# Group norm and channel attention in fp16 halves: norms from weights times T, shared blocks side by side, and another order in the head

## The reference, cut to what matters

```python
x = x + attention(group_norm(x))        # x: 16 images, 192 channels, 48*48 = 2304 pixels
# group_norm: 32 groups of 6 channels, each image alone
qkv = xt @ w_qkv                        # xt: (2304, 192), w_qkv: (192, 576)
q = q / max(sqrt(sum over pixels of q*q), 1e-12)     # by channel; k likewise
k = k * temperature                     # by head; 8 heads of 24 channels
attn = softmax(k^T q)                   # 24 x 24 for each head: sums over the pixels
out = (v @ attn) @ w_out + b_out
```

## Time and profile before

| | us |
|---|---|
| median of 3 runs | 373.13 (372.38 to 373.38) |
| the profiled execution | 374.76 |
| its span in the profile | 372.8 |
| TensorE busy | 331.2 (89%) |
| VectorE busy | 283.2 (76%) |
| ScalarE busy | 235.9 (63%) |
| GpSimd busy | 150.4 (40%) |

### The profile page before, as it was taken

The page is one execution under the profiler, slowest core; times in us unless marked ns, Lnnn a source line. Parts: engine busy times, 40 slices in busy tenths (PEclk is TensorE's granted clock), DMA queues, the critical chain, the costliest instruction groups (busy, mean ns, idle before and its releaser), DMA issues.

```text
span 372.8 us, 9327 instructions
## 1 busy us (share of the span) xinstructions
PE 331.2 (89%) x3724; PEld 233.4 (63%) x3724; DVE 283.2 (76%) x666; ACT 235.9 (63%) x410; POOL 150.4 (40%) x133
## 2 busy tenths in 40 slices
PE   0048856999999999999999999999999999999795
PEld 0036645875778566865777577856686577765452
DVE  4889855887699669986799769966998665359774
ACT  1098489763997299747996399729974699610200
POOL 0079858301970169203950197016920395001000
PEclk9999976899999999999999999999999999999999
DMA  7999900004994279815991499427981563034766
GB/s 235 359 286 246 244 16 3 2 2 139 300 323 132 86 233 326 247 44 137 336 335 44 134 297 338 124 87 226 320 261 45 165 217 88 2 105 150 230 213 192
DMA packets 30826, 67.73 MB, mean 182 GB/s; under 512 B 5504, under 2 KB 12096, under 8 KB 30784
## 3 DMA queue, kind: packets, MB, share of 16 engines
q1 hardware_dynamic: 30544, 66.56, 56.7%
q10 hardware_dynamic: 240, 0.59, 0.6%
HBM read 29.38 MB, written 28.31 MB: 155 GB/s over the span
## 4 chain that ended last, share of the span: by engine, by line
PE 64%; ACT 15%; issue 10%; DVE 5%; DMA 2%; SPq 2%; POOL 1%; ACTq 0%; POOLq 0%
PE u_ps L927 30%; PE g_ps L927 17%; PE s_ps L927 10%; ACT h_sb L543 4%; ACT tok L581 4%; ACT xn L537 3%; PE u_ps L976 2%; DMA wo<-in_L_conv_w_out_dram 2%; PE u_ps L977 2%; ACT h_sb L550 1%; DVE x_sb L855 1%; PE u_ps L979 1%; PE u_ps L978 1%; SPq L354 1%; SPq L359 1%
## 5 line engine op out<-in xcount | busy, mean ns | idle before, releaser
L474 POOL TENSOR_TENSOR l_sb<-xn,h_sb 128x768 f16<-128x768 f32 x63 | 103.8, 1649 | 56.0 <-ACT h_sb L543 55.7
L855 DVE SCALAR_TENSOR_TENSOR x_sb<-u_ps,bias,x_sb 128x384 f32<-128x384 f32 x144 | 85.9, 613 | 24.2 <-PE u_ps L927 24.1
L927 PE MATMUL g_ps<-tok 128*128 128x64 f16 (+1 forms) x864 | 87.1, 241 | 3.4 <-ACT tok L581 2.9
L537 ACT ACTIVATE xn<-x_sb,rb 128x768 f32<-128x768 f32 x63 | 63.6, 1020 | 29.7 <-POOL rb L486 29.7
L581 ACT COPY tok<-u_ps 128x384 f32<-128x384 f32 x144 | 65.0, 485 | 19.8 <-PE u_ps L979 18.6
L927 PEld LDWEIGHTS g_ps<-tok 128*128 128x128 f16 x864 | 57.0, 99 | 28.5 <-ACT tok L581 5.8
L728 DVE BATCH_NORM_STATS2 bnst<-x_sb 128x6 f32<-128x384 f32 x144 | 69.9, 543 | 5.3 <-DMA x_sb<-in_x_dram 5.2
L927 PE MATMUL u_ps<-h_sb,ml 128*128 128x384 f16 (+1 forms) x336 | 73.2, 327 | 0.0
L543 ACT ACTIVATE h_sb<-x_sb,rb 128x768 f16<-128x768 f32 x63 | 64.4, 1022 | 0.0
L976 PE MATMUL u_ps<-id,h_sb 128*128 128x128 f16 x288 | 48.9, 223 | 8.2 <-DVE l_sb L718 7.4
L977 PE MATMUL u_ps<-id,l_sb 128*128 128x128 f16 x288 | 48.9, 223 | 0.0
(11 more groups left out here) (144 smaller groups left out, 567.6 us busy)
## 6 DMA issues: line engine op xcount, KB each, us to landing
x_sb<-in_x_dram SPq DMA_DIRECT2D x48, 384.0 KB, 5.4
out_dram<-x_sb SPq DMA_DIRECT2D x48, 384.0 KB, 2.9
...
```

What stands on the lines that cost most here:

```text
L474: nc.gpsimd.tensor_tensor(l_sb[:, par, t, cols], xn[:, c % XN_RING, :], h_sb[:, par, t, cols], ALU.subtract).then_inc(l_ok, 1)
L537: nc.scalar.activation(xn[:, c % XN_RING, :], xcol(q, t, g * GW, GW), ACT.Identity, bias=rb[:, par, 1, t:t + 1], scale=rb[:, par, 0, t:t + ...
L855: V.scalar_tensor_tensor(out=xs, in0=block_ps(n), scalar=bias[:, t:t + 1], in1=xs, op0=ALU.add, op1=ALU.add).then_inc(out_ok, 1)
L927: return nc.tensor.matmul(dst, lhs, rhs, start=start, stop=stop, skip_group_check=True)
```

## The change

- Norms. With T = G W, the squared norm of column c is the sum over rows of W[r,c] T[r,c]. So VectorE multiplies T by the weights in place in PSUM (`low_t`, second half), ScalarE copies the high part to `pw16` ("p", `high_products`), VectorE takes the remainder ("lo", `low_products`), and TensorE sums over the rows with 24 matmuls of two columns ("squares"), whose one-and-zero operand `side` parts the images. q^T q and k^T k are gone from `scores` (24 matmuls of 96 columns are left), and T's fp16 pair holds the 192 q columns alone.
- Shared blocks. In the middle third the shared rows come first, so results 4, 5, 6 and 7 are shared. The full-width matmuls of 4 and 5 stand ahead of w0 and those of 6 and 7 behind w1, with the halves in one piece: w0's shared rows, z, halves of 4 to 7, w1's shared rows. `gram_weights` does the shared rows first when it is w1. SyncE stores and loads in this order, with a semaphore for each chunk (`stored[t][g]`).
- Head. Value weights are transposed directly behind the first group sums, into a result bank. VectorE makes wml and the value chunks 0 and 1 of pair 1; GpSimd has four steps of low weights instead of eight; the second group sums stand behind slot 17 of the first gram, and the variance ahead of the gram's low part. ScalarE leaves h5, x6 and x7 to phase A of step 0, which has tables of its own (`SECOND_`), with V at slot 10 and M at 13 instead of 8 and 11.

```diff
-PE_B = {0: ["gram"], 2: ["sums"], 4: ["w0"], 6: ["w1"], 12: ["scores"]}
+PE_B = {0: ["gram"], 2: ["sums"], "in 4": ["w0"], "in 7": ["w1"], 11: ["scores"], 13: ["squares"]}
 ACT_A = {0: ["h6"], 2: ["h7"], 4: ["x8"], 6: ["exp", "h8"], 11: ["v"], 14: ["m"]}
-ACT_B = ["x0", "t0", "t1", "t2", "h0", 1, 2, 3, 4, 5, "x6", "x7"]
+ACT_B = ["x0", "x1", "x2", "t2", "t0", "t1", "h0", "h1", "p", "h2", "x3", "x4", "h3", "x5", "h4", "h5", "x6", "x7"]
 POOL_B = ["power", 0, 1, 2, 3, 4, "norms", 5, 6, 7, 8]
 VEC_A = {0: ["soft_in"], 3: ["soft_out"], 7: ["v"], 11: ["m0"], 13: ["m1"], 17: ["stats"]}
-VEC_B = {0: ["gram"], 2: ["var"], 4: ["z"], 6: ["t0", "t1", "t2"], 12: ["norms"], 17: ["spread", "bn", "bn", "bn", "bn"]}
-FIRST_PE_A = {14: ["wv"]}
-FIRST_PE_B = {0: ["gram", "sums"], 2: ["w0"], 7: ["w1", "scores"]}
+VEC_B = {0: ["gram"], 2: ["var"], 3: ["z"], 5: ["t2"], 7: ["t0", "t1"], 10: ["lo"], 13: ["norms"], 17: ["spread", "bn", "bn", "bn", "bn"]}
+FIRST_PE_A = {17: ["sums"]}
+FIRST_PE_B = {0: ["gram"], 2: ["w0"], 7: ["w1", "scores", "squares"]}
 FIRST_ACT_A = {1: [6, 7], 2: [9], 3: [10], 4: [12], 5: [13], 6: [14]}
-FIRST_ACT_B = [0, "x1", "t0", "t1", "t2", "h1", 2, 3, 4, 5, "x6", "x7"]
-FIRST_POOL_B = ["power", 0, 1, 2, 3, 4, "norms", 5, 6, 7, 8]
-FIRST_VEC_A = {17: ["bn"] * 7 + ["stats", "wv"]}
-FIRST_VEC_B = {0: ["gram", "var", "z", "t0", "t1"], 1: ["t2", "bn", "bn", "wo", "norms", "spread", "bn", "bn"]}
+FIRST_ACT_B = ["h0", "h1", "x2", "h2", "t2", "t0", "t1", "x3", "p", "h3", "x4", "h4", "x5"]
+FIRST_POOL_B = ["power", 0, 1, 2, 3, "norms", 4, 5, 6, 7, 8]
+FIRST_VEC_A = {17: ["bn"] * 7 + ["stats"]}
+FIRST_VEC_B = {0: ["var", "gram", "wm", "v0", "v1", "z", "t2", "t0"],
+               1: ["t1", "lo", "bn", "norms", "wo", "spread", "bn", "bn", "bn"]}
 FIRST_BN = (0, 2, 2, 2, 1)
 BN_A = {1: 2, 5: 4, 9: 6, 11: 2}
 BN_EARLY = 4
 POOL_SECONDS = (3, 5)
+BY_VECTOR_1 = 2
+SECOND_PE_A = {3: ["flip"], 10: ["v"], 13: ["m"]}
+SECOND_ACT_A = {0: ["h5"], 1: ["x6"], 2: ["h6"], 3: ["x7"], 4: ["h7"], 5: ["x8"], 6: ["exp"], 7: ["h8"], 12: ["v"], 15: ["m"]}
...
 LAST_PE_A = {0: ["m"]}
-LAST_PE_B = {0: ["gram"], 2: ["w0"], 3: ["w1"], 5: ["scores"], 10: ["flip"], 16: ["v"]}
+LAST_PE_B = {0: ["gram"], 2: ["w0"], 3: ["w1"], 6: ["scores"], 7: ["squares"], 11: ["flip"], 16: ["v"]}
 LAST_ACT_A = {0: ["m"]}
-LAST_ACT_B = ["t0", "t1", "t2", "exp", "v"]
+LAST_ACT_B = ["t2", "t0", "t1", "p", "exp", "v"]
 LAST_POOL_B = ["norms"]
 LAST_VEC_A = {0: ["m0", "m1"]}
-LAST_VEC_B = {0: ["gram"], 2: ["z"], 3: ["t0", "t1", "t2"], 5: ["norms"], 8: ["spread"], 10: ["soft_in"], 12: ["soft_out"],
-              15: ["v"]}
+LAST_VEC_B = {0: ["gram"], 2: ["z"], 3: ["t2", "t0", "t1"], 4: ["lo"], 6: ["norms"], 9: ["spread"], 11: ["soft_in"], 13: ["soft_out"], 15: ["v"]}
...
+    ROWS = [(t, g) for g in range(GROUPS) for t in ((1, 0, 2) if g == 1 else (0, 2, 1))]
+    OUTS = [(t, g * GW + k * BW) for t, g in ROWS for k in (0, 1)]
...
+            def high_products(q):
+                need(act, n_mm, q)
+                for k in (2, 0, 1):
+                    act.wait_ge(pw_ok, 3 * q + T_AT[k])
+                    nc.scalar.copy(pw16[:, k, 0, 0:2 * C], t_ps(k)).then_inc(ph_ok, 1)
...
+            def second_value(c):
+                t, g = CHUNKS[c]
+                if c == 0:
+                    dve.wait_ge(norm, 2 * NORM)
+                    dve.wait_ge(low_ok, 4)
+                V.tensor_scalar(xn[:, c, :], xcol(1, t, g * GW, GW), rb[:, 1, 0, t:t + 1], rb[:, 1, 1, t:t + 1],
+                                ALU.mult, ALU.add).then_inc(xn1_vec, 1)
...
             def norms(q):
+                dve.wait_ge(n_mm, q + 1)
+                V.tensor_scalar(n8[:, :], n_ps[0:HC, :], NORM_EPS ** 2 * NORM_FACTOR, None, ALU.max).then_inc(diag, 1)
...
+                V.tensor_tensor(tq[:, k, 1, :], src[:, 0:C], tq[:, k, 0, :], ALU.subtract).then_inc(tl_ok, 1)
+                dve.wait_ge(tl_ok, 3 * q + T_AT[k])
+                V.scalar_tensor_tensor(out=src[:, 0:2 * C], in0=src[:, 0:2 * C], scalar=W_SCALE, in1=(w1 if k == 2 else w0)[:, 0:2 * C],
+                                       op0=ALU.mult, op1=ALU.mult).then_inc(pw_ok, 1)
+            def low_products(q):
+                for k in (2, 0, 1):
+                    dve.wait_ge(ph_ok, 3 * q + T_AT[k])
+                    V.tensor_tensor(pw16[:, k, 1, 0:2 * C], t_ps(k), pw16[:, k, 0, 0:2 * C], ALU.subtract).then_inc(pl_ok, 1)
...
+            def squares(q):
+                pe.wait_ge(pl_ok, 3 * q + 3)
+                for a in range(4):
+                    c = C - C * (a // 2) + HC * (a % 2)
+                    terms = [(pw16[:, k, i, c:c + P], side[:, k, :]) for k in range(3) for i in (0, 1)]
+                    dst = n_ps.rearrange("p (s b j) -> p s j b", s=2, b=2)[:, a // 2, a % 2, :]
+                    for k, (lhs, one) in enumerate(terms):
+                        last = mm(dst, lhs, one, k == 0, k == len(terms) - 1)
+                last.then_inc(n_mm, 1)
...
+                def lower_weights(n, start):
+                    at = OUTS[n][1]
+                    return mm(block_ps(n), ml1[:, 1, :], h[:, 1, at:at + w], start, not start)
+                def two_halves(start):
+                    dst = block_ps(n)
+                    for b in (0, 1):
+                        mm(dst[C1 * b:C1 * b + C1, :], mh1[:, b, P - P * b:C - P * b], hl[:, b, c:c + w], start)
+                    for k, (m, a) in enumerate(((mh0, h), (mh0, l), (ml0, h))):
+                        for b in (0, 1):
+                            last = mm(dst[C1 * b:C1 * b + C1, :], m[:, b, P:C], a[:, 2 * b, c:c + w], False,
+                                      k == 2 and not start)
+                    return last
...
+                elif n in (4, 16):
+                    lower_weights(n, True)
+                    if n == 4:
+                        bank_free(n + 1)
+                        if sums:
+                            pe.wait_ge(gstep, (q + 2) * GVAR + 1)
+                        lower_weights(n + 1, True)
+                    between()
+                    two_halves(False).then_inc(out_mm, 1)
+                elif n == 5:
+                    two_halves(False).then_inc(out_mm, 1)
+                elif n == 17:
+                    two_halves(True)
+                    lower_weights(n, False).then_inc(out_mm, 1)
                 else:
-                    whole_first = n % 2 == 0
-                    if whole_first:
-                        mm(dst, ml1[:, 1, :], h[:, 1, :], True)
-                    for b in (0, 1):
-                        mm(dst[C1 * b:C1 * b + C1, :], mh1[:, b, P - P * b:C - P * b], hl[:, b, c:c + w], not whole_first)
-                    for k, (m, a) in enumerate(((mh0, h), (mh0, l), (ml0, h))):
-                        for b in (0, 1):
-                            last = mm(dst[C1 * b:C1 * b + C1, :], m[:, b, P:C], a[:, 2 * b, :], False,
-                                      whole_first and k == 2)
-                    if not whole_first:
-                        last = mm(dst, ml1[:, 1, :], h[:, 1, :], False, True)
-                    last.then_inc(out_mm, 1)
+                    two_halves(True)
+                    if n == 7:
+                        between()
+                        for k in (6, 7):
+                            lower_weights(k, False).then_inc(out_mm, 1)
```

More of the change, by code:

```diff
@@ L542, in chunk_high @@
                 t, g = CHUNKS[c]
+                if q == 1 and c == 0:
+                    act.wait_ge(norm, 2 * NORM)
                 nc.scalar.activation(h_sb[:, par, t, g * GW:g * GW + GW], xcol(q, t, g * GW, GW), ACT.Identity,
@@ L962, in transposes @@
                     in_tok(q, j - RING)
+                if q == 0 and j == RING - 1:
+                    pe.wait_ge(wv_ok, 2)
                 if q == 0 and j * P % BW == 0:
@@ new lines, in shared_rows @@
+                def shared_rows():
+                    if not ready:
+                        need(pe, ml_ok, 2 * q)
+                    for k in (range(3, 5) if ready else range(3)):
+                        for b in (0, 1):
+                            dst = s_ps[C1 * b:C1 * b + C1, 0, 0:2 * C]
+                            hi, lo = (q16[:, b, i, P:C] for i in (0, 1))
+                            lhs, rhs = ((hi, wh0), (hi, wl0), (lo, wh0), (z[:, b, P:C], wh1), (z[:, b, P:C], wl1))[k]
+                            last = mm(dst, lhs, rhs[:, :], k == 0, k == 4)
+                    if ready:
+                        last.then_inc(t_mm, 1)
@@ L1166, in _ @@
             small_steps = {"gram": finish_gram, "w0": lambda q: gram_weights(q, False),
-                           "w1": lambda q: gram_weights(q, True), "scores": scores, "flip": flip,
+                           "w1": lambda q: gram_weights(q, True), "scores": scores, "squares": squares, "flip": flip,
                            "v": attn_values, "m": folded_weights}
@@ L1197, in step, with steps_at @@
                     pe.wait_ge(fills, 1)
-                for n in range(NO):
```

(10 more changed lines are left out.)

197 lines of the change are left out of this document (103 added, 94 removed).

## The result

Median 368.91 us (366.01 to 370.11, 5 runs) against 373.13; against all runs of the kernel before on the same chip the ratio is 0.987, 95% interval 0.985 to 0.990. The forecast was 365.5 (359 to 370). The profiled execution took 368.91 us for a span of 367.1.

| | before | forecast | after |
|---|---|---|---|
| results of pair 0 start | 80.96 | 77.6 | 76.53 |
| six passes | 6 x 40.45 | 6 x 39.98 | 39.94, 39.93, **40.92, 40.60**, 39.96, **40.39** |
| tail: results of pair 6 to the end | 49.13 | 47.8 | 48.85 |
| sum against before | | -7.6 | -5.7 |

The account below looks back on a forecast made before the run. TensorE bounded the pass with ScalarE 0.55 us behind; after the change ScalarE would set it. Head -3.4, six passes -2.8 and tail -1.4 sum to -7.6 us, giving a median of 365.5 us (range 359 to 370).

Parts of the forecast that it names:

- The bound of the pass: Ordinary passes: TensorE gains 1.9 us, but ScalarE, 0.55 us behind it, limits the gain to 0.46 us, pass 39.98.
- idle time ahead of the grams: TensorE, before the first gram step of a pass: idle about 1 us, a sign that the forecast is right.
- the six switches: TensorE, results 0 to 17: four switches between whole and half matmuls instead of ten, -0.55 us a pass.
- covered by next to nothing: GpSimd's reciprocal roots, delayed to +21.75: VectorE's spread done at +24.0, TensorE's flip due at +24.07, so no cost.
- The rival that TensorE keeps its gain: Ordinary passes: ScalarE's waits nearly vanish, a pass is 38.96, total 359.4 us; chance 18%.
- the slow products: VectorE's three products take 1653 ns each and delay ScalarE's p copies: pass 43.1, total 384 us; chance 7%.
- the regrouping does nothing: Joining results 4 to 7 saves no time, as TensorE is not the bound; no time of its own, no chance given.
- The queue of transfers: nothing: SyncE's reordered stores and loads: same bytes, VectorE waits only 5.2 us in the run for loads, so no effect.
- Head: Start to pair 0's results: earlier norms and fewer ScalarE chunks start these near 77.6 instead of 80.96, -3.4 us.
- Tail: Last chain: norms free 1.4 us sooner, 1.2 arriving at V, and two switches saved in the last results, -1.4 us.
- the forecast's own case: Whole run: 363 to 368 us with head gain 1 to 5 and product 0.55 to 0.7 us; chance 57%.
- the rival whose head gains nothing: Head: v1 or wm blocks against GpSimd, z comes late; only passes and tail gain, 369 us; chance 13%.

Follow-up runs that it names:

- e4: e1 with the results and their matmuls ordered as in the kernel before (results 4 to 7 not joined); 367.85 us (0.985).
- e3: e1 with chunk h2 moved ahead of the three product copies p in ScalarE's list; 364.22 us (0.975).
- e10: e9 plus chunk h2 ahead of the p copies, chunk 0's values on GpSimd and filler matmuls in the tail; 364.85 us (0.978).
- e9: The changed kernel with all twelve copies of the shared rows of a pass behind its loads in SyncE's queue; 370.31 us (0.993).
- e12: e10 with the results ordered as in the kernel before and not joined; 365.18 us (0.981).
- e1: The changed kernel with SyncE's last four copies of a pass behind the last loads instead of ahead; 367.09 us (0.985).
- e2: The kernel before, as a control, with e1's change of order in SyncE's queue; 373.27 us (1.000).

## Why the prediction was right, and where it was not

- **The bound of the pass: right.** ScalarE's list sets it. Of the 1.8 us by which TensorE's transposes start sooner (+20.89 instead of +22.68), 0.5 shortens the pass and the rest is idle time. Forecast 39.98, undisturbed 39.94. The parts hold: scores, squares, product, p's last copy, idle time ahead of the grams; the six switches were worth 0.41 us of TensorE's time (e4; forecast 0.55). Two small errors cancel: the token copy comes 0.24 us sooner, and the roots' chain, which I had called covered by next to nothing, lacks 0.18 us of cover, at V and not at the flip, since I had not counted the statistics behind the scaling. The rival that TensorE keeps its gain fell with e3 and e4, the slow products with the 566 ns row (against them I had said that the 613 ns add has two operands in PSUM too; it has one); that the regrouping does nothing was right for this kernel, and even in e10 it was worth 0.05 us a pass.
- **"The queue of transfers: nothing" is the step that failed.** I looked at bytes and at VectorE's 5.2 us of waits in the kernel before, and not at how late SyncE's queue already ran: the last load left at +32 to +33 of 40.44 us and landed some 5 us later. In the changed kernel it left at +32.9 to +34.0 of a pass 0.5 us shorter, so a load that is a little slow lands in the path. It cost 2.2 us of the 2.8 forecast for the passes in the profiled execution. The cause is shown by e9 to e12: without the copies ahead of the stores the last load lands at +32.0 to +34.8, and 20 passes with loads have no wait of VectorE for one. In the passes of the other changed kernels with a wait of 0.3 us or more it landed at +36.5 or later. The count of long passes alone would not do, since e1, e3 and e4 had none in 18 either.
- **Head: direction right, sizes off.** The token copy of pair 1 came at 55.87 instead of 57.1. v0 and v1, bounded by 1.1 us each, took 676 ns, and between the norm and that copy ScalarE waited only once, 0.32 us, where I had put in some 1.5 us of waits. From that copy to the results it took 20.66 us, forecast 20.5. But the kernel before itself varies here: 19.40 us at a mean granted clock of 0.83 where the earlier trace rows are from, 18.37 at 0.91 in e2; in the changed kernel it stayed at 1.00. In e9, with the same head, the mean was 0.90 and the stretch took 20.67, so there the low clock is hidden, as forecast. From the last token copy of pair 0 to pair 0's results it was 40.5 and 39.5 us, now 36.2: the head gains 3.3 to 4.3 us; forecast 3.4.
- **Tail: right where the clock stays.** V 1.20 us sooner (forecast 1.2), V to results 5.67 (5.83 before), last results 0.20 shorter (0.2): 47.58 in e1 against 49.13, -1.55 for a forecast of -1.4. The profiled execution lost 1.3 us of it to the slow clock, which no step of mine had: what TensorE saves ahead of V beyond those 1.2 us lengthens its wait there, from 0.96 to 1.85 us.
- **Sum.** e1, where neither disturbance came in its profile, has a span of 364.3, -8.5 against before, for a forecast of -7.6. The changed kernel lost 2.2 us to loads and 1.3 to the clock, and its results of pair 0 start 0.66 us sooner than e1's. The median missed the forecast by 3.4 us: 1.9 in the span, and 1.6 because I took the profiled execution to lie 1.63 above the median as before, while here it is the median. That 368.91 lies inside the range is thus partly luck: it is outside the 363 to 368 given for the forecast's own case, and near the 369 of the rival whose head gains nothing, although the results of pair 0 came 4.4 us sooner here.
